# A graph kernel whose row gathers and VectorE sums run side by side: the sum made tile by tile, and another instruction for the last layer's marks

## The reference, cut to what matters

```
edge_feat = concatenate([h[src], h[dst]])
messages  = relu(edge_feat @ msg_W1 + msg_b1) @ msg_W2 + msg_b2
att       = sigmoid(relu(edge_feat @ att_W1 + att_b1) @ att_W2 + att_b2)
aggregated = segment_sum(messages * att, dst)
```

```
W   = einsum('rb,bio->rio', coefficients, bases)
msg = einsum('ni,rio->rno', x, W)[edge_type, src] * deg_inv[dst]
out = segment_sum(msg, dst) + x @ self_loop
```

## Time and profile before

| what | value |
|---|---|
| median of three runs | 6870.66 us |
| the profiled execution | 6873.15 us |
| its span | 6871.4 us |
| PE busy | 75% |
| DVE busy | 43% |
| ACT busy | 30% |
| POOL busy | 36% |
| first attention pass, gathers | 1060.9 to 2154.4 us |
| second attention pass, gathers | 2238.6 to 3344.8 us |
| last pass, gathers | 5819.4 to 6852.9 us |

### The profile page before, as it was taken

One profiled execution on the slowest core, in us unless ns is written; L12 is line 12 of the kernel. 1 busy time (PEld: TensorE's weight loads), 2 busy tenths in 40 slices (PEclk: granted clock), 3 DMA queues, 4 the chain that ended last, 5 costly groups with the idle time before them and its releaser, 6 DMA issues. The chain is left out here.

```text
span 6871.4 us, 88916 instructions
## 1 busy us (share of the span) xinstructions
PE 5164.6 (75%) x29013; PEld 3487.6 (51%) x29017; DVE 2985.4 (43%) x6890; ACT 2047.6 (30%) x4993; POOL 2506.7 (36%) x2457
## 2 busy tenths in 40 slices
PE   2557757778877777878699899999999997444443
PEld 1435545667766666767544444444444444333333
DVE  6889975555554555555565322112112114111111
ACT  2019974555554554555401101001001013000000
POOL 0000006777774777777300000000000000777776
PEclk7569989998898888999799999999999998555555
DMA  1019984444442444444283553553553543222112
GB/s 59 1 62 329 328 269 122 122 122 122 122 122 80 126 118 118 123 121 123 83 320 130 188 195 134 191 193 132 193 195 132 194 139 159 52 51 51 51 51 56
DMA packets 413670, 941.05 MB, mean 137 GB/s; under 512 B 61345, under 2 KB 270422, under 8 KB 403158
## 3 DMA queue, kind: packets, MB, share of 16 engines
q1 hardware_dynamic: 309846, 670.81, 29.3%
q0 software_dynamic: 103424, 264.92, 14.0%
HBM read 730.94 MB, written 204.56 MB: 136 GB/s over the span
## 5 line engine op out<-in xcount | busy, mean ns | idle before, releaser
L1716 POOL DMA_INDIRECT ring<-rows,stage x1616 | 1708.1, 1057 | 1151.9 <-ACT stage L1751 667.2
L1597 POOL DMA_INDIRECT ring<-rows,stage x808 | 788.5, 976 | 2720.4 <-ACT stage L1581 2474.5
L1303 PE MATMUL ps<-strip,trans_part 128*128 128x512 f16 (+1 forms) x8232 | 1607.3, 356 | 24.0 <-DVE trans_part L1228 24.0
L1303 PEld LDWEIGHTS ps<-strip,trans_part 128*128 128x128 bf16 x8232 | 756.7, 98 | 928.8 <-issue 78.4
L1790 PE MATMUL ps<-here,spread 128*128 x3232 | 1004.9, 438 | 226.5 <-issue 166.6
L1810 PE MATMUL ps<-ring,mark 128*128 128x128 f32 x3232 | 767.7, 327 | 240.0 <-ACT ring L1775 239.7
L1742 DVE SCALAR_TENSOR_TENSOR ring<-ring,dst_part 128x1024 f32<-128x1024 f32 x404 | 496.1, 1228 | 909.7 <-DMA ring<-rows,stage 896.6
L1648 PE MATMUL ps<-ring,mark 128*128 128x128 f32 x1616 | 414.6, 438 | 608.9 <-DMA ring<-rows,stage 607.2
L1810 PEld LDWEIGHTS ps<-ring,mark 128*128 128x128 f32 x3232 | 596.4, 212 | 364.2 <-issue 323.8
L1790 PEld LDWEIGHTS ps<-here,spread 128*128 128x128 f32 x3232 | 609.7, 210 | 333.9 <-issue 263.6
L1648 PEld LDWEIGHTS ps<-ring,mark 128*128 128x128 f32 x1616 | 357.0, 326 | 666.5 <-issue 666.5
(11 more groups left out here) (316 smaller groups left out, 5037.9 us busy)
## 6 DMA issues: line engine op xcount, KB each, us to landing
strip<-adj SPq DMA_DIRECT2D x392, 800.0 KB, 4.3
adj<-piece SPq DMA_DIRECT2D x120, 640.0 KB, 4.0
locs<-loc_rows SPq DMA_DIRECT2D x404, 128.0 KB
ahead<-ahead_piece SPq DMA_DIRECT2D x125, 320.0 KB, 4.2
back<-back_piece SPq DMA_DIRECT2D x125, 320.0 KB, 4.5
sheet<-ahead SPq DMA_DIRECT2D x25, 1600.0 KB, 7.9
sheet<-back SPq DMA_DIRECT2D x25, 1600.0 KB, 8.0
ring<-rows,stage POOLq DMA_INDIRECT x2424, 2.5
```

The lines of the kernel that those rows point to most:

```text
L1303: last = eng.matmul(k.ps[:, b, 0:cols], part[:, (step * NW + w) % TABLES, m, t * D:(t + 1) * D], strip[:, at % RING, c0:c0 + cols], start= ...
L1597: eng.indirect_dma_start(ring[:, t, :], None, rows, bass.IndirectOffsetOnAxis(stage[:, t:t + 1], 0)).then_inc(s_full[q], 16)
L1716: eng.indirect_dma_start(ring[:, t, :], None, rows, bass.IndirectOffsetOnAxis(stage[:, t:t + 1], 0)).then_inc(s_full[g % RING], 16)
```

## The change

In `attention_pass` the sum of a quad is made by four instructions of 128x256, one per tile, in place of one of 128x1024. The last of the four tells the semaphore, and the wait before the dot products stays. In `last_pass` the marks are made by scalar_tensor_tensor (add 0.0, then is_equal) in place of tensor_tensor (is_equal), with the same operands and output.

```diff
@@ last_pass, VectorE
-                eng.tensor_tensor(mark[:, q, :, :], k.tile_no[:, 0:P].unsqueeze(1).to_broadcast([P, QUAD, P]),
-                                  words[:, bass.ds(at, QUAD), D_LOC].unsqueeze(2).to_broadcast([P, QUAD, P]),
-                                  ALU.is_equal).then_inc(s_mark, 1)
+                eng.scalar_tensor_tensor(mark[:, q, :, :], k.tile_no[:, 0:P].unsqueeze(1).to_broadcast([P, QUAD, P]), 0.0,
+                                         words[:, bass.ds(at, QUAD), D_LOC].unsqueeze(2).to_broadcast([P, QUAD, P]),
+                                         ALU.add, ALU.is_equal).then_inc(s_mark, 1)
@@ attention_pass, VectorE
-                quad = ring[:, tiles_of(g), :]
-                eng.scalar_tensor_tensor(quad, quad, 1.0, part[:, g % PARTS, :, :], ALU.mult, ALU.add).then_inc(s_add, 1)
+                for j in range(QUAD):
+                    row = ring[:, g % RING * QUAD + j, :]
+                    last = eng.scalar_tensor_tensor(row, row, 1.0, part[:, g % PARTS, j, :], ALU.mult, ALU.add)
+                last.then_inc(s_add, 1)
```

## The result

Six runs of the changed kernel have a median of 6834.9 us (6828.52 to 6839.0), six of the kernel before 6888.02 (6859.9 to 6900.23). The ratio is 0.9928, with a 95% interval of 0.9906 to 0.9949: 53 us by the medians, 59 forecast. The profiled executions differ less: 6873.15 before, 6833.86 after, spans 6871.4 and 6832.2, so 39 us. It reaches for what it waits for 0.13 us after its start. A pause is idle time of GpSimd between two gathers above the usual 0.305 us.

A forecast was written before the change was run, and what follows sets the result against it. POOL's uninterrupted gathers were taken to bound the attention passes. 6873.15 - 59 (sum) + 0.5 (DVE) + 1 (marks) = 6815.7 us profiled, 6814 as median; forecast's own range 6770 to 6840, 8 in 10 range 6762 to 6890.

The forecast's parts named there:

- The bound: Attention passes: POOL's gathers and their gaps set the time; holds add 0.44 us a quad, 178 us over 404 quads.
- The rule of the hold: A gather reaching 0.13 us after its start waits from about 0.16 into a DVE instruction until that instruction's end.
- The pieces' time: Attention sum on DVE: four pieces of 0.42 us, 0.345 apart, take 1.46 us, 0.23 more a quad.
- DVE's longer work costs nothing: Attention pass: DVE's load of 3.2 to 3.4 us a quad hides behind POOL's 5, about 0.5 us in all.
- The third rival: Attention sum: POOL cannot get in between pieces, gathers wait for the fourth's end; +46 us, 6917 us, chance 0.05.
- The walk's four quads: Attention gathers followed through four changed quads: holds of 0.15, 0.43, 0.08 and 0.49 us, 0.29 a quad.
- the 0.30 taken: Attention pass: hold time per quad assumed after the change, in us, against 0.44 before; saves 59 us.
- the second rival: Attention pass: each quad's first gather falls into the mark, 0.70 us a quad; +100 us, 6971 us, chance 0.11.
- The first rival: Attention pass: spread and mark take over the sum's holds, or the skill's inference holds; no change, 6871 us, chance 0.20.
- the mean of 1020 ns: Attention gathers (line 1716): expected mean duration after the change, down from 1057 ns.
- The marks' form: Last pass: marks by scalar_tensor_tensor take the same time and also hold gathers; +1 us, bounds -26 to +15.
- Wrong altogether if POOL waits for PE: Attention pass: the forecast's own condition for failing, POOL having to wait for PE or ACT; no size given.

The follow-up runs named there:

- att_marks_scalar_2: Changed kernel with the attention pass's marks by four tensor_scalar instructions of 128x128, second timing: 6815.37 us, ratio 0.9759 to the kernel before at 6981.6.
- att_marks_scalar: Changed kernel with the attention pass's marks by four tensor_scalar instructions of 128x128, first timing: ratio 1.0089 to the kernel before at 7288.25.
- both_marks_scalar: Changed kernel with the marks of both passes by four tensor_scalar instructions of 128x128: 7418.2 us, ratio 1.0077 to the kernel before at 7364.36.

## Why the prediction was right, by its steps

The bound, POOL's unbroken row of gathers, was right on the chip where it was made, and all that moved there moved in the gathers' mean. The rule of the hold stood with two limits. It starts about 0.16 us into a DVE instruction (0.20 for tensor_scalar), ends with it, and lets the gather through before the next piece, except for the 15 of att_marks_scalar_2 that waited out two pieces more. And the prediction put it on DVE instructions at large, which is too wide: tensor_reduce with one SBUF input held none. The Trainium skill's inference (SBUF — State Buffer, "Who interferes with whom") that tensor_tensor does not stall descriptor making is contradicted by the last pass before, where it held 56 gathers for 26 us. The sentence in that section that an instruction with at most one SBUF input, outside the two-port modes, does not contend agrees with 0 of 394; the spread and the tensor_scalar marks have one tensor input and held gathers, which fits only if they ran in such a mode, and no run shows the mode.

The pieces' time, 1.43 measured for 1.46, was right, and that DVE's longer work costs nothing holds where POOL does not pause. The third rival is out for this profile, with no hold by a piece over 0.275 us; in one later run its mechanism came for those 15 gathers.

The size. The walk's four quads, times 101, would be sum 43 us, spread 24, marks 43, dots 5: 116 in all (121 with the 0.30 taken). Measured are 49, 11, 63 and 15: 144 by the same count, 0.36 a quad. The term that was too small is the marks': they held 192 gathers in 404 quads, where the walk had one in four quads; 103 of these stood in the place that the second rival named, the first gather. In the sum the term had two thirds of its weight, 43 us for 62.6; the dots' had a third, 5 for 15, and the spread's twice too much, 24 for 11. The first rival named the same thing: of the 116 us that sum and spread gave up, marks and dots took 74. So the profiled executions give 39 us where 59 were forecast, and each pass is 15 and 22 us shorter, not 30. By the medians it is 53, but no trace explains the 14 us between, and part of this nearness is luck: against 6870.66, the median that the forecast started from, 6834.9 is 36 us less; the three later runs of before were slower (6884.08 to 6900.23). The median lies in the range of 6770 to 6840, near its end. (6815.7 less 2.5 is 6813, not 6814; nothing hangs on it.) The second rival's full price, 0.70 a quad, came in no profile, and the mean of 1020 ns was missed by 14.

The marks' form: forecast +1 us, measured 3 less in the profile and 1.0003 alone, within what the bounds of -26 to +15 allow and with no effect to be seen.

What the prediction did not see is that the bound depends on where the kernel runs. On three of four later chips GpSimd waits for TensorE's late releases, the shorter holds turn into pauses, and the same change gives 1.001 on one, its main part 1.005 on another. "Wrong altogether if POOL waits for PE" was its own condition, and there it applies. The profile of before gave no sign of it.

## What to carry to other kernels

Where GpSimd's gathers run back to back and bound a stage, look for the long VectorE instructions that run beside them: what each costs is the rest of it after the gather has reached, so cut them short. Here every instruction with two SBUF inputs held gathers, and tensor_scalar with one tensor input did too; only tensor_reduce did not. Cutting one moves the phase, and other instructions take holds over: here two thirds of what the first cut gave up, and all of it at the step from halves to quarters. So count holds by instruction after each cut. And time such a change on more than one chip: the same edits that gained 0.7 to 2.4% on one kind gained nothing or lost up to 0.9% on the other.

## What the runs showed of the hardware that I had not expected

A gather that reaches during the first 0.16 us of a VectorE instruction with two SBUF inputs is served first, and the DVE instruction is then up to 0.07 us longer (1.297 at most for 1.226, in the profile before). The hold by tensor_scalar begins at 0.20 and not at 0.16 (in att_marks_scalar none of 3 that reached between 0.14 and 0.17 was held, one of 5 between 0.17 and 0.20, 72 of 73 after; but in the last pass of both_marks_scalar 6 of 60 between 0.14 and 0.17 were). A gather that reaches within 8 ns of a piece's end can miss it and wait for the end of the row of pieces, 0.67 us later (15 times in att_marks_scalar_2, in no other profile). A four-way cut of a two-input sum and a two-way cut gave the same time, 6876.3 and 6872.96. On three chips TensorE's semaphore came late in 208 to 276 of 808 cases in every kernel profiled (592 to 680 us in total), against 0 of 808 in six other profiles; and the last pass, a hardware loop of 25 rounds, had 26 to 37 pauses of 3.6 to 5.9 us (medians) there, and none elsewhere.
